# A shared expert's second product, taken from two reduced-precision parts instead of full fp32, with GpSimd making one of the parts

## What is computed

```python
def _expert(x, Wg, Wu, Wd):
    return jax.nn.silu(x @ Wg.T) * (x @ Wu.T) @ Wd.T
shared = _expert(x, Wg_s, Wu_s, Wd_s)          # x: 8 x 512 x 256, hidden width 512
logits = jnp.einsum('bsh,eh->bse', x, Wr) + rb
scores, idx = jax.lax.top_k(jax.nn.sigmoid(logits), 2)
out = shared
for e in range(8):
    out = out + cw[..., e:e + 1] * _expert(x, Wg[e], Wu[e], Wd[e])
h = h + out                                     # x is the layernorm of h
```

## Time and profile before

| | us |
|---|---|
| median of three runs (1157.01 to 1158.73) | 1158.5 |
| the profiled execution | 1163.81 |
| its span in the profile | 1161.9 |
| PE busy | 1116.7 (96%) |
| PE weight loads busy | 718.5 (62%) |
| DVE busy | 916.8 (79%) |
| ACT busy | 584.2 (50%) |
| GpSimd busy | 394.3 (34%) |

### The profile page before, as it was taken

One profiled execution on the slowest core, in us unless ns is written; L12 is line 12 of the kernel. 1 busy time (PEld: TensorE's weight loads), 2 busy tenths in 40 slices (PEclk: granted clock), 3 DMA queues, 4 the chain that ended last, 5 costly groups with the idle time before them and its releaser, 6 DMA issues.

```text
span 1161.9 us, 22261 instructions
## 1 busy us (share of the span) xinstructions
PE 1116.7 (96%) x6090; PEld 718.5 (62%) x6091; DVE 916.8 (79%) x1571; ACT 584.2 (50%) x973; POOL 394.3 (34%) x508
## 2 busy tenths in 40 slices
PE   9999999999999999989999999969999999999996
PEld 5654333333333333477777787757888888888885
DVE  4788888888888887678888888777777777777774
ACT  4445777777777777631233222432444444444442
POOL 2002621011111101214345443353555555554553
PEclk9998999999999999989999999999999999999998
DMA  7887333332333322041244541122333333333332
GB/s 232 273 273 259 92 89 88 93 99 81 95 85 90 103 72 87 1 164 42 68 109 109 100 98 39 38 47 78 55 55 54 51 56 52 51 53 54 54 55 32
DMA packets 109714, 105.37 MB, mean 91 GB/s; under 512 B 42464, under 2 KB 97904, under 8 KB 109648
## 3 DMA queue, kind: packets, MB, share of 16 engines
q1 hardware_dynamic: 92704, 85.38, 26.2%
q0 software_dynamic: 16960, 19.38, 10.5%
HBM read 64.88 MB, written 39.68 MB: 90 GB/s over the span
## 4 chain that ended last, share of the span: by engine, by line
PE 73%; DVE 10%; issue 3%; POOL 3%; ACT 1%; another core or an unknown queue 0%; DMA 0%; POOLq 0%; DVEq 0%; ACTq 0%
PE mix_pairs L73 20%; PE pv L688 11%; PE by_key L675 10%; PE by_query L666 9%; PE mix_made L1874 9%; PE mix_turn L1861 3%; POOL kept_table L1130 3%; PE mix_made L1282 2%; PE mix_made L1270 2%; PE by_query L709 2%; PE mix_turn L1841 1%; PE mix_pairs L1308 1%; PE mix_made L1253 1%; DVE mix_stats L1462 1%; DVE k_mix_u L1472 1%
## 5 line engine op out<-in xcount | busy, mean ns | idle before, releaser
L762 DVE TENSOR_REDUCE k_neg_max<-by_query 128x2 f32<-128x1024 f32 x240 | 282.8, 1220 | 48.4 <-PE by_query L666 45.2
L823 ACT ACTIVATE k_wu_e<-by_key 128x512 f32<-128x512 f32 x512 | 270.1, 600 | 64.9 <-PE by_key L675 64.8
L675 PE MATMUL by_key<-k_wg_e 99*128 99x512 bf16 x512 | 175.1, 384 | 2.8 <-PEq L147 2.4
L1818 POOL DMA_INDIRECT out_rows<-x_y,k_slot x72 | 114.0, 1583 | 156.1 <-PE mix_turn L1841 104.6
L666 PE MATMUL by_query<-k_wg_e 96*128 96x512 bf16 x480 | 144.7, 382 | 0.0
L1918 ACT ACTIVATE x_gate<-mix_pairs 128x512 f32<-128x512 f32 x72 | 43.0, 597 | 196.8 <-PE mix_pairs L73 196.8
L688 PE MATMUL pv<-k_wu_e,k_wd_e 128*17 128x512 f32 x1024 | 134.5, 598 | 0.3 <-ACT k_wu_e L823 0.3
L73 PE MATMUL mix_pairs<-w_short,x_T 128*128 x288 | 120.8, 419 | 2.2 <-issue 2.2
L1874 PEld LDWEIGHTS mix_made<-x_wd,x_acts_T 128*128 128x128 f32 x864 | 111.2, 188 | 7.4 <-ACT x_acts_T L1941 0.9
L73 PE MATMUL mix_pairs<-w_short,x_rest 128*128 x288 | 113.9, 396 | 0.0
L1874 PE MATMUL mix_made<-x_wd,x_acts_T 128*128 128x256 f32 x864 | 112.6, 279 | 0.7 <-ACT x_acts_T L1941 0.7
(11 more groups left out here) (251 smaller groups left out, 1960.8 us busy)
## 6 DMA issues: line engine op xcount, KB each, us to landing
k_wg_e<-kept_qk SPq DMA_DIRECT2D x384, 64.0 KB, 2.3
kept_qk<-k_qk_parts SPq DMA_DIRECT2D x32, 384.0 KB, 3.4
kept_v<-k_v_ones SPq DMA_DIRECT2D x8, 544.0 KB, 5.3
k_wd_e<-kept_v SPq DMA_DIRECT2D x32, 136.0 KB, 2.7
k_wu_e<-in_xT SPq DMA_DIRECT2D x8, 512.0 KB, 4.6
kept_heads<-k_wd_e SPq DMA_DIRECT2D x8, 512.0 KB, 3.0
k_heads_in<-kept_heads SPq DMA_DIRECT2D x8, 512.0 KB
k_wg_e<-in_wg_e SPq DMA_DIRECT2D x8, 512.0 KB, 4.7
```

The source lines that it names most:

```text
L675: pe.matmul(by_key[:, key_bank(job), :], k_rows[0:SROWS, g, h, kt * P:(kt + 1) * P], q_rows[0:SROWS, g, h, :], start=True, stop=True).then ...
L762: dve.tensor_reduce(neg_max[:, g % 2, 2 * n:2 * n + 2], by_query[:, bank:bank + 2, :], AX.X, ALU.max, negate=True).then_inc(query_read, 1)
L823: act.activation(probs[:, key_tile(j) // 2 * G + j // 2 % G, j % 2, :], by_key[:, key_bank(job), :], ACT.Exp, scale=float(HD) ** -0.5).the ...
L1818: pool.indirect_dma_start(out=dram["out"], in_=y[:, r % 2, :], in_offset=None, compute_op=ALU.add, out_offset=bass.IndirectOffsetOnAxis(ap ...
```

## The change

In steps 1 to 7 the shared expert's second product, for batch b - 1, is made of fp32r parts (`shared_down_parts`): for each of 16 pairs of a token tile and a hidden part, three fp32r matmuls on 256 columns. Step 8 keeps `shared_down` in fp32.

- The down matrix's two parts are made once, in step 0: ACT rounds it (128x1024), DVE subtracts (128x1024), after the last store of attention's heads has landed.
- The activations' short part is made by ACT in two halves of 128x1024 (`shorten_acts`), the first after `silu` 1, the second after `silu` 3.
- The rest of the activations is made by GpSimd in two halves of 128x1024 (`rest_of_acts`), in place over the activations. Both halves stand between L1111 and the power for the second layernorm.
- PE goes over the hidden halves outermost: 24 matmuls on the first half, then 24 on the second, each half behind a wait for GpSimd.
- The parts take the place of the down matrices of experts 2 to 5. `load_expert` no longer loads these; SP loads them in step 7, after PE's product of batch 6, and the two of before in step 8. The waits for loads count accordingly.
- Four semaphores of the class row are merged into one, `cls_products`, with counts 1 to 4.

```diff
+EARLY_DOWN = 2
@@ stage_mix, places
+        with ExitStack() as alias:
+            gate_rest = alias.enter_context(nc.sbuf_tensor("gate_rest", [P, FC, S], FP32))
         gate = sb("mix_gate", [P, FC, S], FP32)
+        gate_short, wd_s_parts = mem["gate_short"], (mem["wd_s_short"], mem["wd_s_rest"])
@@ sync
-                for name in ("wg_e", "wu_e", "wd_e") if e < E - 2 else ("wg_e", "wu_e"):
+                for name in ("wg_e", "wu_e", "wd_e") if e < EARLY_DOWN else ("wg_e", "wu_e"):
...
-            def load_late():
-                sp.wait_ge(ev["gate_made"], FC * B)
-                for e in (E - 2, E - 1):
+            def load_late(free, count, which):
+                sp.wait_ge(ev[free], count)
+                for e in which:
...
+                if this and not nxt:
+                    load_late("down_made", 2 * b, range(EARLY_DOWN, E - 2))
                 if prev and this:
                     store_out(b, par)
@@ gpsimd
+            def rest_of_acts(j, half):
+                pool.wait_ge(ev["acts_shortened"], 2 * j + half + 1)
+                some = slice(2 * half, 2 * half + 2)
+                pool.tensor_tensor(short(gate_rest[:, some, :]), gate[:, some, :], gate_short[:, some, :],
+                                   ALU.subtract).then_inc(ev["acts_cut"], 1)
...
                     pool.tensor_tensor(rows, rows, h[:, :, :], ALU.add).then_inc(ev["ud_done"], 1)
+                    if prev:
+                        rest_of_acts(b - 1, 0)
+                        rest_of_acts(b - 1, 1)
                     inverse_deviation(b, 2)
@@ scalar
+            def shorten_acts(j, half):
+                act.wait_ge(ev["act_done"], FC * j + 2 * half + 2)
+                act.wait_ge(ev["down_made"], 2 * j)
+                some = slice(2 * half, 2 * half + 2)
+                act.activation(short(gate_short[:, some, :]), gate[:, some, :], ACT.Copy).then_inc(ev["acts_shortened"], 1)
...
+                if this and prev:
+                    shorten_acts(b - 1, 0)
                 if prev:
                     silu(b - 1, 2)
...
                     silu(b - 1, 3)
+                if this and prev:
+                    shorten_acts(b - 1, 1)
...
+            act.activation(short(wd_s_parts[0][:, :, :]), mem["wd_s"][:, :, :], ACT.Copy).then_inc(ev["shared_shortened"], 1)
             batches(act, step)
@@ tensor
+            def shared_down_parts(j):
+                for half in range(2):
+                    pe.wait_ge(ev["act_done"], FC * j + FC - 1)
+                    pe.wait_ge(ev["acts_cut"], 2 * j + half + 1)
+                    if j == 0:
+                        pe.wait_ge(ev["w_s_cut"], 3)
+                    for t in range(TT):
+                        for m in (2 * half, 2 * half + 1):
+                            mm = split_products(pe, pairs[:, 0, t // 2, (t % 2) * D:(t % 2 + 1) * D],
+                                                [part[:, m, t * P:(t + 1) * P] for part in (gate_short, gate_rest)],
+                                                [part[:, m, :] for part in wd_s_parts],
+                                                start=(m == 0 and t % 2 == 0), stop=(m == FC - 1 and t % 2 == 1))
+                        if half and t % 2:
+                            mm.then_inc(ev["down_made"], 1)
...
-                if prev:
+                if this and prev:
+                    shared_down_parts(b - 1)
+                elif prev:
                     shared_down(b - 1, 0)
                     shared_down(b - 1, 1)
@@ vector
+                if not prev:
+                    dve.wait_ge(ev["shared_shortened"], 3)
+                    dve.wait_ge(mem["heads_stored"], 16 * B)
+                    dve.tensor_tensor(short(wd_s_parts[1][:, :, :]), mem["wd_s"][:, :, :], wd_s_parts[0][:, :, :],
+                                      ALU.subtract).then_inc(ev["w_s_cut"], 1)
                 if this:
                     dve.wait_ge(ev["ud_done"], 2 * b + 2)
@@ program
-            alias.enter_context(nc.sbuf_tensor("down_place", [P, E - 2, FC, D], FP32))
+            alias.enter_context(nc.sbuf_tensor("down_place", [P, EARLY_DOWN, FC, D], FP32))
+            for name, shape in (("wd_s_rest", [P, FC, D]), ("wd_s_short", [P, FC, D]), ("gate_short", [P, FC, S])):
+                mem[name] = alias.enter_context(nc.sbuf_tensor(name, shape, FP32))
```

More of the change, by code:

```diff
@@ L1072, in step @@
                                            max_val=16 * (1 + TT * B))
-                    load_late()
+                    load_late("gate_made", FC * B, (E - 2, E - 1))
                     sp.wait_ge(slots_out[0], 16 * (1 + TT * B))
@@ L1176, in step @@
                 if 1 <= b <= EARLY:
-                    act.wait_ge(mem["expert_in"][(b - 1) // 2], 16 * 3)
+                    act.wait_ge(mem["expert_in"][(b - 1) // 2], 16 * (3 if b <= 2 * EARLY_DOWN else 2))
                     shorten_weights(act, mem, b - 1)
                 if last:
-                    act.wait_ge(mem["experts_in"], 16 * (3 * (E - 3) - 2))
+                    act.wait_ge(mem["experts_in"], 16 * 2 * (E - 3))
                     shorten_weights(act, mem, 5)
@@ L1408, in beside @@
                     pe.wait_ge(ev["cls_copied"], 2)
-                    class_product(cls_early, cls_state, mem["m2_T"], D, "cls_y")
+                    class_product(cls_early, cls_state, mem["m2_T"], D, "cls_products")
                 if (g, j) == (3, 4):
@@ L1419, in class_up @@
                 pe.wait_ge(ev["cls_copied"], 3)
-                class_product(cls_ps[0], cls_u2_T, mem["wr_T"], E, "cls_logits")
+                class_product(cls_ps[0], cls_u2_T, mem["wr_T"], E, "cls_products")
                 for bank, w in ((1, mem["wg_s"]), (2, mem["wu_s"])):
@@ L1425, in class_up @@
                                            start=(c == 0), stop=(c == 1))
-                mm.then_inc(ev["cls_up"], 1)
+                mm.then_inc(ev["cls_products"], 1)
             def class_down():
@@ L1431, in class_down @@
                     mm = pe.matmul(cls_ps[3][:, 0:D], cls_act_T[:, m, :], mem["wd_s"][:, m, :], start=(m == 0), stop=(m == FC - 1))
-                mm.then_inc(ev["cls_down"], 1)
+                mm.then_inc(ev["cls_products"], 1)
             attention[2](pe, beside)
@@ L1623, in class_end @@
             def class_end():
-                dve.wait_ge(ev["cls_y"], 1)
+                dve.wait_ge(ev["cls_products"], 1)
                 dve.tensor_tensor(cls_h, cls_h, cls_early[:, 0:D], ALU.add).then_inc(ev["cls_h2"], 1)
@@ L1656, in class_bias @@
             def class_bias():
-                dve.wait_ge(ev["cls_logits"], 1)
+                dve.wait_ge(ev["cls_products"], 2)
                 dve.tensor_tensor(cls_probs[:, 0, :], cls_ps[0][:, 0:E], mem["rb_row"][:, :], ALU.add).then_inc(ev["cls_biased"], 1)
@@ L1682, in class_add @@
             def class_add():
-                dve.wait_ge(ev["cls_down"], 1)
+                dve.wait_ge(ev["cls_products"], 4)
                 dve.tensor_tensor(cls_h, cls_h, cls_ps[3][:, 0:D], ALU.add).then_inc(ev["cls_done"], 1)
@@ L1878, in tensor @@
         for e in range(3):
-            pe.wait_ge(mem["expert_in"][e], 16 * 3)
-        pe.wait_ge(mem["experts_in"], 16 * 3 * (E - 3))
+            pe.wait_ge(mem["expert_in"][e], 16 * (3 if e < EARLY_DOWN else 2))
+        pe.wait_ge(mem["experts_in"], 16 * (3 * E - 6 - EARLY_DOWN))
         pe.wait_ge(mem["lists_made"], 2)
@@ L1946, in scalar @@
         act.wait_ge(mem["lists_made"], 2)
-        act.wait_ge(mem["experts_in"], 16 * 3 * (E - 3))
+        act.wait_ge(mem["experts_in"], 16 * (3 * E - 6 - EARLY_DOWN))
         shorten_down(0, 0)
```

8 lines of the change are left out of this document (4 added, 4 removed).

## The result

The changed kernel takes **1176.6 us** (median of four runs, 1171.49 to 1177.23) against 1158.6 us before (four runs, one more than at the start): a ratio over all runs of **1.0147** (the two medians alone give 1.0155), with a 95% interval from 1.0122 to 1.0172, which is 14 to 20 us. By the medians it is 18 us slower. 1174 was forecast, with a range from 1157 to 1182.

The account below looks back on a forecast made before the run. PE's product and DVE's u2 were taken to end each step almost together, 0.17 us apart. 11.9 (scans) + 1.0 (step 0) + 3.7 (clock) - 1.0 (product) = 15.6 us, giving 1174 us after carrying over 5.3; range 1157 to 1182.

Parts of the forecast that it names:

- Reading of the bound: End of a mixing step: PE's product ends the wait for u2, DVE's u2 would end it 0.17 us earlier.
- Part 2: First scans, steps 1 to 7: each waits for GpSimd's whole first-half subtraction, 11.9 us together.
- Part 6: Before y's product: longer PE idle time lowers its clock, 0 to 1.5 us in each of five steps; 3.7 counted.
- The rival of that name: PE's clock falls in all five steps and stays down into the second product: 7.5 and some 3 more; chance 0.10.
- Part 1: PE's second product: 5.60 us for 6.91, but only 0.17 us a step free before DVE's u2, 1.0 over six steps.
- Part 3: GpSimd's second half and the second layernorm's power: the subtraction is just out of the power's way; nothing counted.
- Part 4: Step 0: DVE's subtraction of the down matrix starts the sum late and delays u2 by 1.0 us.
- Part 5: Steps 7 and 8: down matrices of experts 2 to 5 load late but arrive in time; nothing counted.
- Carrying over the 5.3 us: The profiled execution of before lay 5.3 us over the runs' median; that difference was kept in turning 1179.4 into 1174.

Follow-up runs that it names:

- late_rest: Changed kernel, but GpSimd waits for both of DVE's hidden halves before its first subtraction of the rests; 1162.7 against 1162.5 us, ratio 1.0006.
- before_order: Kernel before, fp32 product kept, with u2 normalised in the middle of `place` and the next first layernorm's power behind four scatters; 1158.8 against 1159.7 us, ratio 0.9991.
- best_power: late_rest plus u2 normalised mid-`place`, PE's short-part matmuls first, and the next first layernorm's power behind four scatters; 1155.9 against 1163.6 us, ratio 0.9934.
- awake: Changed kernel plus nine unused fp32r matmuls of 512 columns ahead of y's product in steps 1 to 7; 1174.4 us, ratio 1.0105.
- fp32_product: Changed kernel with the second product back in fp32, GpSimd's subtractions keeping place and size; 1178.2 us, ratio 1.0117.
- before_again: The kernel before, unchanged, profiled a second time; 1159.6 us.
- cut_later: Changed kernel with DVE's step 0 subtraction of the down matrix moved behind the normalising of u2; 1176.0 us, ratio 1.0127.
- quarters: Changed kernel with each of GpSimd's two subtractions cut into four instructions of 128x256; 1176.9 against 1165.6 us, ratio 1.0097.

## Why the prediction was right

The forecast was 15.6 us more, and 18.0 were measured, 17.7 of them in the profile up to step 7. By its parts:

- **Reading of the bound** (u2 on DVE only 0.17 us ahead of PE's product): right. The fp32r product gave 0.06 us a step in late_rest (34.88 for 34.94), and before_order, best_power and late_rest show the two ends apart.
- **Part 2, the scans wait for GpSimd's whole instruction, 11.9 us**: the mechanism is right, shown by late_rest. The size was a little high: the scans read 1.97 us too much in step 1, 1.60 to 1.63 in steps 2 to 5, 0.74 and 0.76 in steps 6 and 7, 9.9 in all. In step 4 the scan was issued 1.83 us before GpSimd's end and lost 1.63; in step 1 it was 2.17 and 1.97, in step 6 0.94 and 0.74. So 0.20 us of a blocked scan's time runs beside the instruction it waits for, and the sum should have had that less seven times, 1.4 us; the other 0.6 is that GpSimd ended a little earlier before the scans than was worked out. The rows of L916 held this already: it was issued 1.41 us before L1108's end and read 1.27 too much, so it did not take quite its usual time on top, as the prediction reads it.
- **Part 6, the clock, 3.7 us** ("half of the five"): this was mis-sized. It fell in all five steps of the changed kernel's profile, and by awake it made 6.3 us there. The rival of that name, priced at 7.5 and 3 more, is what happened, but at 6.3: a step of the changed kernel is 1.1 to 1.4 us longer than one of awake, and the fall did not last into the second product (the clock is at 1.00 from 657). Step 1 has no term at all in this part: the scan's wait took PE's idle time there from 2.87 to 5.10 us, and y's product from 5.40 to 6.75, 1.35 more.
- **Part 1, the product**: 5.9 us rather than 5.6 (5.8 in late_rest): 118 ns for each matmul, and a first one that takes 0.3 with the clock still low. Its worth of 0.17 us a step was 0.06 with the scans on time (late_rest) and 0.2 to 0.5 with the scans late (fp32_product).
- **Part 3, no cost**: right. Subtraction and power had 1.5 us between them, and PE didn't wait for the second half. The clock's cost (part 6) reaches u2 through this stretch: y's product, slowed, kept DVE's sum (L1508, at 656.14) waiting 1.33 us.
- **Part 4, 1.0 us in step 0**: right where the clock holds, with 0.9; in the profiled execution it was hidden, for another cause than the change.
- **Part 5, the loads, no cost**: right by late_rest, which has them all.
- **Carrying over the 5.3 us** between the profiled execution of before and the median: right, and before_again shows what they were. ACT's unnamed waits in step 8 vary from execution to execution. (The trace of before has two of them, 10.1 us, and not three; for a third wait, of 4.17, it names PE.)

So the mechanism was right, but that the time came within 3 us is in part luck: 2.0 us too much for the scans stood against 2.6 too little for the clock and 1.35 for step 1. The profile's 17.7 us are 9.9 for the scans, 6.3 and 1.35 for the clock in the five steps and in step 1, and 1.55 for step 0, less 1.4 that was given back where the sum had 1.0. The 1.4 is what is left over; no run splits it.

## What to carry to other kernels

Before you put work on GpSimd, look at what DVE runs at that moment: in these traces an operation with two SBUF inputs, a scan too, waits for all of GpSimd's instruction (2.9 us for 1.28), and pieces of a quarter took the wait only from 1.63 to 1.33 us; beside DVE's operations that read PSUM the same subtraction cost nothing. When two engines reach a join almost together, a saving on one is worth nothing until the other is moved too, and each move must be followed into the queues behind it (here a power behind six scatters). And an idle time of 2 us on PE costs more than 2 us, if the clock falls in the product that follows: here up to 1.5 us more.

## What the runs showed of the hardware that was not expected

- PE's clock isn't settled by the idle time ahead of the product alone. With 1.9 to 2.2 us of idle before y's product in steps 2 to 7 it fell in 14 of 18 steps (after, cut_later, quarters, fp32_product). It never fell at 0.6 or 1.3 to 1.5 us there, and in fp32_product it held once after 3.28 us. In step 0, ahead of the class token's product, PE idles 1.29 us in all 14 profiles, and there the clock fell in six (after, late_rest, awake, fp32_product, best_power, before_again) and held in eight (before and cut_later among them). What decides between them stays open.
- A GpSimd subtraction of 128x1024 takes 2.36 to 2.42 us, four of 128x256 take 2.82 together (654.72 in quarters): some 0.14 us for each of three cuts.
- The wait that ACT shows in step 8 for something unnamed was 10.1 and 5.0 us in two executions of the kernel before, and anything from none to 12.2 us in those of the changed kernel and its variants. Its cause was not looked for.
